# Gated top-k MLP in split float32: x of blocks 1 to 3 transposed by VectorE, a new gate for the odd weight subtractions, and 56 transposes of the identity at the start

## What is computed

```python
xn = layernorm(x)                                  # (2048, 1024)
s = silu(xn @ wa_gate.T)                           # (2048, 2752)
s[the 1376 smallest |s| of each row] = 0
a = (s * (xn @ wa_up.T)) @ wa_down.T
g = silu((silu(xn @ wb_gate.T) * (xn @ wb_up.T)) @ wb_down.T)
out = x + a * g
```

## Time and profile before

| | us |
|---|---|
| three runs | 2883.02, 2885.12, 2886.37 (median 2885.12) |
| the profiled execution | 2883.35 |
| its span, first to last instruction | 2881.6 |
| block 0, to the first transpose of block 1 | 735.2 |
| blocks 1 and 2, from first transpose to first transpose, each | 713.4 |
| block 3, from its first transpose to the end | 719.4 |

### The profile page before, as it was taken

The page is one execution under the profiler, slowest core; times in us unless marked ns, Lnnn a source line. Parts: engine busy times, 40 slices in busy tenths (PEclk is TensorE's granted clock), DMA queues, the critical chain, the costliest instruction groups (busy, mean ns, idle before and its releaser), DMA issues.

```text
span 2881.6 us, 31393 instructions
## 1 busy us (share of the span) xinstructions
PE 2856.6 (99%) x12832; PEld 2379.1 (83%) x12832; DVE 1662.0 (58%) x2060; ACT 1223.0 (42%) x1226; POOL 656.8 (23%) x282
## 2 busy tenths in 40 slices
PE   7999999999999999999999999999999999999999
PEld 6888888888888888888888888888888888888887
DVE  3135877976402588797321168878732217787861
ACT  3335887433222466632122256663212225666320
POOL 5665443024544100000054410000005440000000
PEclk9999999999999999999999999999999999999999
DMA  6767887569422455556532255555643225555554
GB/s 225 247 239 278 282 287 278 190 242 325 156 95 97 164 197 191 190 194 226 199 124 99 96 177 189 190 195 197 228 181 129 97 91 186 191 195 197 189 212 168
DMA packets 99886, 549.95 MB, mean 191 GB/s; under 512 B 10976, under 2 KB 10976, under 8 KB 52960
## 3 DMA queue, kind: packets, MB, share of 16 engines
q1 hardware_dynamic: 99808, 548.97, 53.7%
HBM read 449.31 MB, written 99.61 MB: 190 GB/s over the span
## 4 chain that ended last, share of the span: by engine, by line
PE 95%; ACT 1%; issue 1%; DMA 1%; POOL 0%; DVE 0%; POOLq 0%; DVEq 0%; SPq 0%
PE ps L349 33%; PE ps L404 11%; PE ps L405 11%; PE ps L407 11%; PE ps L429 10%; PE ps L431 10%; PE ps L430 10%; ACT signs L504 1%; DMA w_raw<-w_b 1%; PE ps L466 1%; PE ps L389 1%; POOL w_split L640 0%; ACT w_split L488 0%; DVE stats L687 0%; DMA prods<-x 0%
## 5 line engine op out<-in xcount | busy, mean ns | idle before, releaser
L640 POOL TENSOR_TENSOR w_split<-w_raw,w_split 128x1024 fp32r<-128x1024 f32 (+1 forms) x242 | 575.4, 2380 | 1738.6 <-ACT w_split L488 1513.1
L349 PE MATMUL ps<-w_split,hid_ring 128*128 128x512 f32 x4160 | 944.9, 389 | 0.9 <-issue 0.9
L349 PEld LDWEIGHTS ps<-w_split,hid_ring 128*128 128x128 f32 x4160 | 780.2, 188 | 164.2 <-issue 2.2
L739 DVE TENSOR_SCALAR_CACHE_REDUCE ranks<-key_buf,cand 128x2752 int16<-128x2752 f32 x248 | 762.9, 3076 | 5.4
L504 ACT ACTIVATE signs<-key_buf,cand 128x2752 bf16<-128x2752 f32 x248 | 642.2, 2590 | 193.6 <-DVE cand L748 184.4
L488 ACT ACTIVATE w_split<-w_raw 128x1024 fp32r<-128x1024 f32 (+1 forms) x242 | 251.7, 1043 | 699.2 <-DMA w_raw<-w_a 545.7
L404 PE MATMUL ps<-w_split,xnT 128*128 128x512 f32 (+1 forms) x1408 | 541.5, 385 | 0.0
L405 PE MATMUL ps<-w_split,xnT 128*128 128x512 f32 (+1 forms) x1408 | 540.8, 384 | 0.0
L429 PE MATMUL ps<-xnT,w_split 128*128 128x512 f32 x1376 | 535.8, 389 | 3.5 <-POOL w_split L640 3.5
L430 PE MATMUL ps<-xnT,w_split 128*128 128x512 f32 x1376 | 535.4, 389 | 0.0
L431 PE MATMUL ps<-xnT,w_split 128*128 128x512 f32 x1376 | 535.4, 389 | 0.0
(11 more groups left out here) (69 smaller groups left out, 1233.8 us busy)
## 6 DMA issues: line engine op xcount, KB each, us to landing
w_split<-split SPq DMA_DIRECT2D x280, 1024.0 KB, 4.8
w_raw<-w_a SPq DMA_DIRECT2D x160, 512.0 KB, 3.5
split<-w_split SPq DMA_DIRECT2D x64, 1024.0 KB, 6.9
split<-w_stage SPq DMA_DIRECT2D x22, 1024.0 KB, 6.5
w_raw<-w_b SPq DMA_DIRECT2D x42, 512.0 KB, 4.6
w_stage_raw<-wd_b SPq DMA_DIRECT2D x22, 512.0 KB, 4.9
w_raw<-wd_a SPq DMA_DIRECT2D x22, 512.0 KB, 5.4
prods<-x SPq DMA_DIRECT2D x16, 512.0 KB, 5.8
```

Of the source, the lines that this page charges most:

```text
L349: ins = pe.matmul(ps[:, 2 * t + half, :], h, w[:, half * TB:(half + 1) * TB], start=(first and n == 0), stop=(last and n == 1))
L640: pool.tensor_tensor(w_lo[q][:, 0:w], w_raw[q][:, 0:w], w_hi[q][:, 0:w].bitcast(F32), ALU.subtract).then_inc(lo_ready, 1)
L739: dve.tensor_scalar(ranks[:, :], keys[:, t, :], cand_f[:, t:t + 1], 0.0, ALU.is_lt, ALU.add, accum_out=counts[:, t:t + 1]).then_inc(sel_st ...
```

## The change

In words, with the names of the new code:

- **x of blocks 1 to 3 is transposed by VectorE.** The 96 transposes on TensorE go away. In A-down of the block before, DVE now takes the statistics of token tiles 0 and 1 after tile 6 and of 2 and 3 after tile 7 (`STATS_AT`), applies them after tile 8 (`NORM_AT`), then makes 64 transposes of 32 partitions x (4 x 2 x 32), 11 after each tile from 9 (9 after tile 14), into `x_feat`, which are columns 1024 to 2047 of `prods`. ACT makes the high parts from there (`xn_high`), four after tiles 15 to 18, two when tiles 18 and 19 are done, and two after the last; DVE the low parts (`xn_low`), three after tiles 16 to 18, three after the loop and two at the start of the next block.
- **Layout and order of the chunks.** `xnT` is [KC, 2, TB], so that the ring of hidden chunks lies on chunks 0 to 3, and the chunks are used in the order 4, 5, 6, 7, 2, 3, 0, 1 (`K_ORDER`); the weight tiles are loaded in that order. TensorE now waits for `xn_ready` at every chunk, and for `ad_free` at the first product of a bank. `norm_apply` does the second half of the features first.
- **The gate of the odd subtractions.** The search rounds are tabulated in `ROUNDS_AFTER`; the rounds themselves and their places are the same. An odd tile's subtraction waits for the first of its chunk's rounds, where it waited for the round after the chunk's last. For chunks with one round that is the same number; for chunks 2, 6, 10, 14 and 18 of block 0, which have two, it is one round earlier.
- **Start.** TensorE transposes the identity 56 times (`WARM`) into the last bank, ahead of x.

```diff
+TWO_AFTER = (2, 6, 10, 14, 18)
+K_ORDER = (4, 5, 6, 7, 2, 3, 0, 1)
+STATS_AT = 6
+NORM_AT = 8
+X_SQUARES_AT = 9
+X_SQUARES_STEP = 11
+X_PARTS_AT = 15
+WARM = 56
...
-        xnT = at("xnT", [2, KC, TB], F32R, xn_at)
+        xnT = at("xnT", [KC, 2, TB], F32R, xn_at)
+        x_feat = prods[:, :, H:2 * H].rearrange("p t (k n) -> p t k n", k=KC // NT)
...
-                for k in range(KC):
-                    if k % (KC // 2) == 0:
-                        pe.wait_ge(xn_normed, b * (2 * NT) + (k // (KC // 2) + 1) * NT)
-                    pe.wait_ge(ad_free, b * NT + (k // 2 + 1))
-                    for t in range(NT):
-                        ins = pe.transpose(ps[:, k, t * P:(t + 1) * P], prods[:, t, k * P:(k + 1) * P], ident[:, :])
-                    ins.then_inc(xn_turned, 1)
+                if b == 0:
+                    for n in range(WARM):
+                        pe.transpose(ps[:, KC - 1, n % NT * P:(n % NT + 1) * P], ident[:, :], ident[:, :])
+                    for n, k in enumerate(K_ORDER):
+                        if n % (KC // 2) == 0:
+                            pe.wait_ge(xn_normed, NT if n == 0 else 2 * NT)
+                        for t in range(NT):
+                            ins = pe.transpose(ps[:, n, t * P:(t + 1) * P], prods[:, t, k * P:(k + 1) * P], ident[:, :])
+                        ins.then_inc(xn_turned, 1)
...
-                chunk = (m - B0 - 4) // 2 + (m - B0) % 2
-                if B0 + 4 <= m < BD0 and chunk < PAIRS * GROUPS:
-                    pool.wait_ge(cand_ready, ROUNDS_FIRST + chunk + (chunk + 1) // PAIRS + 1)
+                if B0 + 4 <= m < BD0:
+                    pool.wait_ge(cand_ready, ROUNDS_AFTER[(m - B0 - 4) // 2].start + (m - B0) % 2 + 1)
...
+            def xn_low(b, n, src=None):
+                k = K_ORDER[n]
+                dve.wait_ge(xn_hi, b * KC + (n + 1))
+                dve.tensor_tensor(xnT[:, k, 1, :], x_feat[:, k // 2, k % 2, :] if src is None else src,
+                                  xnT[:, k, 0, :].bitcast(F32), ALU.subtract).then_inc(xn_ready, 1)
...
-                        if j == LOOP4 * RING:
-                            norm_stats(b + 1, 0)
-                            norm_stats(b + 1, 1)
-                        elif j == LOOP4 * RING + 1:
-                            norm_stats(b + 1, 2)
-                            norm_stats(b + 1, 3)
-                            norm_rstd(b + 1)
+                        if STATS_AT <= j < STATS_AT + 2:
+                            for t in (2 * (j - STATS_AT), 2 * (j - STATS_AT) + 1):
+                                norm_stats(b + 1, t)
+                            if j == STATS_AT + 1:
+                                norm_rstd(b + 1)
+                        elif j == NORM_AT:
+                            norm_apply(b + 1)
+                            dve.wait_ge(xn_normed, (b + 2) * (2 * NT))
+                        for square in x_squares[max(0, j - X_SQUARES_AT) * X_SQUARES_STEP:max(0, j - X_SQUARES_AT + 1) * X_SQUARES_STEP]:
+                            ins = turn_x_squares(*square)
+                            if square == x_squares[-1]:
+                                ins.then_inc(xn_squares, 1)
+                        if j > X_PARTS_AT:
+                            xn_low(b + 1, j - X_PARTS_AT - 1)
                 if not last_block:
-                    norm_apply(b + 1)
+                    for n in range(NJ - 1 - AHEAD - X_PARTS_AT, 6):
+                        xn_low(b + 1, n)
```

More of the change, by code:

```diff
@@ L51 @@
 ROUNDS_FIRST = 2
-ROUNDS_GROUP = 5
-ROUNDS_B = ROUNDS_FIRST + ROUNDS_GROUP * GROUPS
+TWO_AFTER = (2, 6, 10, 14, 18)
+ROUNDS_AFTER = []
+for chunk in range(PAIRS * GROUPS):
+    first = ROUNDS_AFTER[-1].stop if chunk else ROUNDS_FIRST
+    ROUNDS_AFTER.append(range(first, first + (2 if chunk in TWO_AFTER else 1)))
+ROUNDS_B = ROUNDS_AFTER[-1].stop
 ROUNDS_AT = (0, 1, 3, 4)
@@ L204, in build @@
         xn_turned = sem("xn_turned")
+        xn_squares = sem("xn_squares")
         xn_hi = sem("xn_hi")
@@ L428, in b_tile @@
                         lo = w_lo[q][:, n * P:(n + 1) * P]
-                        pe.matmul(ps[:, bank, :], hi, xnT[:, 0, k, :], start=(first and n == 0), stop=False)
-                        pe.matmul(ps[:, bank, :], hi, xnT[:, 1, k, :], start=False, stop=False)
-                        ins = pe.matmul(ps[:, bank, :], lo, xnT[:, 0, k, :], start=False, stop=(last and k == KC - 1))
+                        pe.matmul(ps[:, bank, :], hi, xnT[:, k, 0, :], start=(first and n == 0), stop=False)
+                        pe.matmul(ps[:, bank, :], hi, xnT[:, k, 1, :], start=False, stop=False)
+                        ins = pe.matmul(ps[:, bank, :], lo, xnT[:, k, 0, :], start=False, stop=(last and k == KC - 1))
                     ins.then_inc(tiles_done, 1)
@@ L509, in run @@
                         hi(b, m)
-                for k in range(KC):
-                    act.wait_ge(xn_turned, b * KC + (k + 1))
-                    act.activation(xnT[:, 0, k, :], ps[:, k, :], ACT.Copy).then_inc(xn_hi, 1)
+                    for n, k in enumerate(K_ORDER):
+                        act.wait_ge(xn_turned, n + 1)
+                        act.activation(xnT[:, k, 0, :], ps[:, n, :], ACT.Copy).then_inc(xn_hi, 1)
                 if not first_block:
@@ L557, in run @@
                         hi(b, B0 + 3)
-                for i in range(GROUPS):
-                    group(i)
-                silu_b(GROUPS, 0)
+                for c, rounds in enumerate(ROUNDS_AFTER):
+                    silu_b(c)
+                    hi(b, B0 + 2 * c + 4)
+                    for n in rounds:
+                        count(n)
+                        if n == rounds.start:
+                            hi(b, B0 + 2 * c + 5)
+                silu_b(NJ - 2)
                 for j in range(AHEAD):
@@ L717, in norm_apply @@
                 dve.wait_ge(ln_step, n * NORM_STEPS + NORM_STEPS)
-                for half in (slice(0, H // 2), slice(H // 2, H)):
+                for half in (slice(H // 2, H), slice(0, H // 2)):
                     for t in range(NT):
@@ L756, in hid_lo_part @@
                         dve.tensor_tensor(hid_ring[:, s, 1, :], src, hid_ring[:, s, 0, :].bitcast(F32), ALU.subtract).then_inc(hid_lo, 1)
[L758 to L762 removed]
+                if b == 0:
+                    for n in range(KC):
+                        xn_low(0, n, ps[:, n, :])
+                else:
+                    for n in (6, 7):
+                        xn_low(b, n)
                     last_outputs(b - 1)
```

88 lines of the change are left out of this document (48 added, 40 removed).

## The result

| us | before | after |
|---|---|---|
| median of 6 runs | 2885.45 | 2873.22 |
| lowest to highest | 2883.02 to 2887.36 | 2871.62 to 2875.06 |
| span of the profiled execution | 2881.6 | 2869.9 |

The change saves 12.2 us, a ratio of 0.9959 (95% interval 0.9947 to 0.9970). The forecast was 2874. The six executions of the changed kernel lie in pairs near 2871.7, 2873.2 and 2875.0; the profiled one (2871.75) is of the lowest pair.

What follows compares the result with a forecast made beforehand. TensorE, busy 99% of the span, was taken as the bound. The terms -10.5 - 4.9 - 0.8 + 4.0 + 1.1 sum to -11.1 us, from a median of 2885.12 to 2874 us; range 2868 to 2880.

Steps and rivals of the forecast that it cites:

- (a): Three boundaries between blocks: 96 transposes and the slow first product after them leave TensorE's path, -10.5 us.
- (b): B products of block 0: five TensorE waits for a POOL subtraction go with the new gate number, -4.9 us.
- Rival 4: The gate: a second wait is as late, so the five waits stay, -6, 2879 us; chance 0.05.
- (c): Start: identity transposes may make x's 32 transposes run fast; bounds 0 and -1.5, middle taken, -0.8 us.
- Row and page: Start: trace row has the clock falling 4.0 us after last work (0 gain); skill page's example 5.2 us (-1.5).
- (d): A-down of block 0: VectorE's new transposes make low parts late for TensorE, +4 us, ends 2 and 6.5.
- the stepping: A-down of block 0: VectorE's queue followed against due times; low parts 11 and 12 late, sum 3.0 or 5.4 us.
- the collision: A-down of block 0: POOL's next subtraction gets ahead of low part 12, 2.4 us more wait.
- rival 2: VectorE's transposes cost 0.5 us each, their destination having three strides; net -4 to -5, 2880 us; chance 0.14.
- Rival 1: VectorE's new work costs nothing in block 0 and the clock holds: -16.9, 2868 us; chance 0.18.
- (e): From block 0 into block 1: TensorE waits for POOL's subtraction for weight tile 2, +1.1 us.

Runs made afterwards that it cites:

- gate_only: The kernel before with the new gate number for POOL's odd subtractions and nothing else: 2878.81 us, ratio 0.9980.
- old_gate: The changed kernel with the old lines of the gate: 2877.47 us.
- after_again: The changed kernel run once more, with no edit: 2874.94 us.
- out_pool_2: The changed kernel with x added by POOL for two token tiles instead of three, by VectorE for the other two: 2874.81 us.
- wait_low2: The changed kernel with VectorE's last two low parts of x and its add held, in blocks 1 to 3, until POOL subtracted for weight tile 2: 2874.03 us.
- all_four: The changed kernel with 88 identity transposes, a gate on tile B0+3, VectorE's wait for weight tile 2, and x one tile later: 2866.50 us.
- no_warm: The changed kernel without the 56 transposes of the identity (WARM = 0): 2873.22 us.
- gate_b3: The changed kernel with POOL's subtraction for weight tile B0+3 gated on the end of the first round: 2873.33 us.
- extra_5: The changed kernel with 5 more transposes into unused bytes beside the 11 of each iteration, in blocks 1 and 2 only: 2889.36 us.

## Why the prediction was right

- **What bounds the kernel**: work on TensorE counts in full. (a) came out at 10.5 us, to the tenth, since the seam has neither the transposes nor the slow first product.
- **(b)** was 4.9 of 4.9 by the trace, and gate_only and old_gate show it from both sides. Rival 4, the second wait, fell with them.
- **(c)** was 0.7 of 0.8, but the middle of two bounds is luck as a forecast of one execution: the traces give 0 to 0.7. Row and page had differed, and the runs sided with the row in that the clock fell before x was transposed. It gave 0.7 all the same, where the row's bound was 0, as the clock was back at full by 18 us, ahead of the last transposes: the granted clock between 18 and 20 us was 1.00 here, and 0.69 in after_again, which gave 0. The granted clock was at half between 15 and 17 us in eight traces of eight, after rests of 3.6 to 5.2 us. Of the Trainium skill's page TensorE: Matmul & The Clock Gate (Part 1) the statement that idleness sends the engine back to half holds; its example of 5.2 us after the last matmul is no lower limit. Nor are the 4.0 us of the earlier trace rows: in out_pool_2 the last of the 56 ends at 9.7 us, and the granted clock between 12 and 13 is 0.55.
- **(d)** is the term that was mis-sized in the first trace, 2.8 for 4.0, and the step that made it so is the middle I took between 3.0 and 5.4. Both sums of the stepping are borne out: the form without the collision has 2.8 to 3.5 us in four traces and the one with it 5.4 to 5.9 in five. I treated a choice of two as one number. The parts hold: a transposition cost 0.449 us where 0.453 was worked out, rival 2 (0.5 us, for the third stride) fell, and the late low parts were 11 and 12, then a few tenths each. Rival 1, "DVE keeps up", fell in block 0 and was true in blocks 1 and 2. VectorE had 58% busy time before and 61% after, and TensorE waited for it all the same.
- **(e)** was 1.0 of 1.1, and wait_low2 shows the mechanism.
- **What was missing** is the wait at 281 us, +0.8. The prediction looked for new meetings of POOL and VectorE only in the stretches that the diff names. The subtraction for B0+3 has no gate, in either kernel, and in the kernel before it started 0.6 us behind the last small step of a round, only because a load was late. I did not ask what it would meet if it came a microsecond sooner. In the sum it hides most of what (d) was too large by, so that 11.6 against 11.1 is closer than the terms are.
- The rule of the Trainium skill (page VectorE: DVE Perf Modes, section Rules for kernel authors) to leave 128 x 128 transposes to TensorE would have cost 10.5 us here to save the 3.8 of (d) and (e), which all_four shows to be avoidable. The rule looks at the transposition, and what decided here was which engine had time.

## What to carry to other kernels

Here one engine was busy for 99% of the span, and moving work off it paid the work's full length (10.5 us), less what the receiving engine lost by it. So place such work with care: step the receiving engine through its queue against the due times of what stands behind, instead of reading its busy share. Where two engines hold each other up, as VectorE's two-input operations and POOL's subtractions do here (2.84 us where 0.69 is the time alone), small pieces that others wait for should have a gate, or be out of reach, or they will be hit by chance in some executions. And a term that is a matter of chance should be forecast as two values with a chance each.

## What the runs showed of the hardware

- The clock can fall in the middle of a kernel in which TensorE is busy for 99% of the span. In no_warm TensorE waited 2.9 us for low part 12, and the window after it shows 10 products in 3.3 us at a granted clock of 0.57, where the same window of gate_b3 has 16. In extra_5 it fell to half behind a wait of 2.3 us in block 1, and in gate_b3 a wait of 3.0 us at low part 12 left it at full; so did those of 3.0 to 3.3 us in out_pool_2, wait_low2 and after_again. The length of the wait alone does not decide. Nor did the fall cost what the slow products suggest: block 1 of extra_5, with it, loses 7.6 us in A-down, and block 2, without it, 7.6 too; no_warm has 5.9 in (d) where the other traces with the collision have 5.4 to 5.7. While TensorE is slow, VectorE catches up, and the waits behind are shorter or gone. The windows (busy us and products that touch the window, granted clock, DMA share, GB/s) of no_warm, extra_5 and gate_b3:

```profile
682.80:686.10 3.30, 3.30 (x10) 0.57 0.74 313
```

```profile
1418.10:1421.10 3.00, 3.00 (x7) 0.50 0.59 249
```

```profile
681.00:684.00 3.00, 2.91 (x13) 1.00 1.03 426
```

- A VectorE operation on 128 x 4 elements with two SBUF inputs (COPY_PREDICATED), 0.16 us long, took up to 2.39 us beside a POOL subtraction; VectorE's transposes in SBUF did not grow beside one (11 in 4.92 to 4.95 us in all iterations of the changed kernel, with POOL in block 0 and without it in blocks 1 and 2).
